# Edits at four block boundaries of a graph network with routed experts

## What is computed

```python
def _L1_gnn_ref(x, edge_index, edge_weight, W_conv, b_conv, W_lin, b_lin):
    n = x.shape[0]
    src, dst = (edge_index[0], edge_index[1])
    loop = jnp.arange(n, dtype=edge_index.dtype)
    src_f = jnp.concatenate([src, loop])
    dst_f = jnp.concatenate([dst, loop])
    w = jnp.concatenate([edge_weight, jnp.ones((n,), x.dtype)])   # the loops: an identity
    deg = jax.ops.segment_sum(w, dst_f, num_segments=n)
    dinv = jnp.where(deg > 0, jax.lax.rsqrt(deg), 0.0)
    norm = dinv[src_f] * w * dinv[dst_f]
    agg = jax.ops.segment_sum((x @ W_conv)[src_f] * norm[:, None], dst_f, num_segments=n) + b_conv
    return agg @ W_lin + b_lin
# L1_ffn: top-2 of 8 experts for each row; hidden 2048 with gelu; the two results mixed by gates
```

## Time and profile before

| what | us |
|---|---|
| median of three runs | 2176.21 (2175.12 to 2176.47) |
| the profiled execution | 2176.15 |
| its span | 2174.3 |
| PE busy | 1678.3 (77%) |
| DVE busy | 873.4 (40%) |
| POOL busy | 710.0 (33%) |
| ACT busy | 572.8 (26%) |
| seams between the blocks | 791.8, 1062.4, 1466.9 |

### The profile page before, as it was taken

The page is one execution under the profiler, slowest core; times in us unless marked ns, Lnnn a source line. Parts: engine busy times, 40 slices in busy tenths (PEclk is TensorE's granted clock), DMA queues, the critical chain, the costliest instruction groups (busy, mean ns, idle before and its releaser), DMA issues. The chain is left out here.

```text
span 2174.3 us, 25832 instructions
## 1 busy us (share of the span) xinstructions
PE 1678.3 (77%) x7876; PEld 1089.5 (50%) x7877; DVE 873.4 (40%) x2140; ACT 572.8 (26%) x1576; POOL 710.0 (33%) x803
## 2 busy tenths in 40 slices
PE   5111100269889978888898999979999999999998
PEld 4000000124335557777544444557777777777775
DVE  7101021124674579999897565660000000000002
ACT  0000001011112369999411111332212111222222
POOL 4777777700000039999730211012000000007004
PEclk8555555679999999999998999989999999999999
DMA  7000000000730030000204000447450440042003
GB/s 219 2 2 2 2 2 2 2 1 0 266 110 10 24 75 0 0 0 0 49 0 136 1 1 0 155 185 244 156 220 19 174 174 19 16 172 67 19 19 104
DMA packets 76132, 143.93 MB, mean 66 GB/s; under 512 B 21797, under 2 KB 23333, under 8 KB 71849
## 3 DMA queue, kind: packets, MB, share of 16 engines
q1 hardware_dynamic: 49415, 118.44, 15.6%
q0 software_dynamic: 18976, 10.95, 2.2%
q10 hardware_dynamic: 7682, 13.87, 1.9%
HBM read 107.61 MB, written 35.56 MB: 66 GB/s over the span
## 5 line engine op out<-in xcount | busy, mean ns | idle before, releaser
L2176 PEld LDWEIGHTS et_ps_h<-ex_turned,arena 128*128 128x128 f32 x3072 | 348.8, 193 | 17.1 <-issue 17.1
L2176 PE MATMUL et_ps_h<-ex_turned,arena 128*128 128x128 f32 x3072 | 349.1, 276 | 5.9 <-issue 5.9
L384 POOL DMA_INDIRECT sorted_edges<-fa_records,fa_edge_slot x313 | 309.6, 989 | 124.9 <-issue 101.6
L2186 PE MATMUL et_ps_y<-arena,et_hidden_t 128*128 x768 | 337.5, 592 | 0.0
L2086 DVE TENSOR_SCALAR ex_turned<-et_ps_t,ex_ln_g,ex_ln_b 128x128 f32<-128x128 f32 x96 | 32.8, 403 | 584.1 <-PE et_ps_t L2156 584.1
L1165 POOL TENSOR_SCALAR ad_row<-iota,ad_edges 128x128 fp32r<-128x128 f32 x360 | 235.6, 671 | 27.6 <-PE ad_ps L1235 23.8
L2186 PEld LDWEIGHTS et_ps_y<-arena,et_hidden_t 128*128 128x128 f32 x768 | 142.2, 190 | 160.7 <-issue 160.7
L517 PE MATMUL fa_banks<-arena 120*128 120x120 bf16 x216 | 33.4, 245 | 195.2 <-issue 195.2
L1214 ACT ACTIVATE ad_row_high<-ad_row,ad_edges 128x128 fp32r<-128x128 f32 x432 | 168.4, 390 | 8.1 <-POOL ad_row L1165 6.8
L1234 PE MATMUL ad_ps<-ad_to,ad_row_high 128*128 128x320 f32 x432 | 144.5, 345 | 32.2 <-ACT ad_row_low L1215 32.2
L2057 POOL DMA_INDIRECT xn_rows<-slot_out,from_slots x10 | 12.1, 1214 | 475.2 <-POOLq L2054 472.5
(11 more groups left out here) (421 smaller groups left out, 2245.0 us busy)
## 6 DMA issues: line engine op xcount, KB each, us to landing
arena<-L_ffn_W SPq DMA_DIRECT2D x16, 4096.0 KB, 13.5
slot_rows<-fa_zeros SPq DMA_DIRECT2D x1, 7424.0 KB, 26.3
slot_out<-fa_zeros SPq DMA_DIRECT2D x1, 7168.0 KB, 45.6
slot_out<-et_y ACTq DMA_DIRECT2D x24, 256.0 KB
et_rows_in<-slot_rows ACTq DMA_DIRECT2D x24, 256.0 KB, 2.7
sorted_edges<-fa_records,fa_edge_slot POOLq DMA_INDIRECT x313
arena<-x SPq DMA_DIRECT2D x1, 2240.0 KB
neighbour<-fa_Wv SPq DMA_DIRECT2D x10, 224.0 KB
```

The lines of the kernel that those rows point to most:

```text
L384: nc.gpsimd.indirect_dma_start(g.sorted_edges, bass.IndirectOffsetOnAxis(ap=self.edge_slot[0:rows, e:e + 1], axis=0), self.records[0:rows, ...
L2176: last = pe.matmul(ps_h[:, f % 2, i, :], x.weights[:, at:at + P], turned[:, k, :], start=(k == 0), stop=(k == KD - 1))
L2186: last = pe.matmul(ps_y[:], hidden_t[:, i, :], x.weights[:, bass.ds(buffer * (2 * HALF) + (HALF + i * D), D)], start=(i == 0), stop=(i == ...
```

## The change

- The first 24 chunks of the sorted edges are loaded by SP at the end of flow_attention, after its last stores, into a part of `arena` that is free then (`g.first_edges`); the load in the adjacency is gone, and `field` reads the new place for the first 8 groups. `first_loaded` now belongs to `g`.
- The ten identity adds stand behind the columns of group 1, ahead of the first sum, which waits for them (`chain`).
- ACT's part of the adjacency is written out for all 144 groups.
- `clear` sorts the numbers first.
- `buffer_of` is gone; PE computes `e % 2` in a register. The five semaphores that PE raised at its start are raised by SP.
- The output tiles' two DMAs are issued by two queues: of each tile, SP stores one part and ACT's queue the other, in alternation.

```diff
@@ Memory.clear
-        first = self.numbers[0]
-        for i, number in enumerate(self.numbers):
-            if i + 1 == len(self.numbers) or self.numbers[i + 1] != number + 1:
+        numbers = sorted(self.numbers)
+        first = numbers[0]
+        for i, number in enumerate(numbers):
+            if i + 1 == len(numbers) or numbers[i + 1] != number + 1:
                 self.nc.gpsimd.sem_clear(range(first, number + 1))
-                first = self.numbers[min(i + 1, len(self.numbers) - 1)]
+                first = numbers[min(i + 1, len(numbers) - 1)]
@@ flow_attention, SP
             sp.wait_ge(s["side_stored0"], 32 * T)
             sp.wait_ge(s["side_stored1"], 32 * T)
             sp.wait_ge(positions.s["zeroed"], 32)
+            sp.wait_ge(g.scattered, 16 * (FULL + 1))
+            sp.dma_start(g.first_edges[:], g.sorted_edges.rearrange("(p s) f -> p s f", p=P)[:, 0:FIRST * CHUNKS]
+                         ).then_inc(g.first_loaded, 16)
@@ adjacency
         def field(t, c, f):
             s = t * CHUNKS + c
+            if isinstance(t, int) and t < FIRST:
+                return g.first_edges[:, s, f:f + 1]
@@ adjacency, SP (POOL, DVE and ACT wait for g.first_loaded)
-            sp.dma_start(edges[:, 0:cut], sorted_edges[:, 0:cut]).then_inc(first_loaded, 16)
             sp.dma_start(edges[:, cut:], sorted_edges[:, cut:]).then_inc(loaded, 16)
@@ adjacency, DVE
+            def add_loops():
+                for b in range(T):
+                    own = weights[0:NT, b, b * NT:(b + 1) * NT]
+                    last = v.tensor_tensor(own, own, g.ident[0:NT, 0:NT], ALU.add)
+                last.then_inc(chain, 1)
 ...
                 last.then_inc(columns_made, 1)
+                if t == 1:
+                    add_loops()
 ...
+                if t == 0:
+                    dve.wait_ge(chain, 1)
                 dve.wait_ge(added, t + BUFS)
 ...
             dve.wait_ge(added, NG + BUFS)
-            for b in range(T):
-                own = weights[0:NT, b, b * NT:(b + 1) * NT]
-                last = v.tensor_tensor(own, own, g.ident[0:NT, 0:NT], ALU.add)
-            last.then_inc(chain, 1)
-            dve.wait_ge(chain, 1)
@@ adjacency, ACT
-            staggered(Steps(act, chain), 0, nothing, scale, nothing, NG, BUFS)
+            for t in range(NG):
+                scale(t, t % BUFS)
@@ nodes, DVE
-            c.link(v.tensor_scalar(x.buffer_of[:], x.expert_of[:], 1, None, ALU.bitwise_and))
@@ expert_tiles, SP
+            sp.sem_inc(s["rows_ready"], 1)
+            sp.sem_inc(s["hidden_ready"], 2)
+            sp.sem_inc(s["rows_turned"], 1)
+            sp.sem_inc(s["rows_loaded"], 16)
+            sp.sem_inc(s["tiles_done"], 1)
 ...
-            for t in range(0, T, 2):
+            for t in range(T):
+                cut = ROW_CUTS[t % 2]
                 sp.wait_ge(s["summed"], t + 1)
-                for cut in ROW_CUTS:
-                    sp.dma_start(A["out"][tile_rows(cut, t)], g.x[cut, t, :]).then_inc(s["out_stored"], 16)
+                sp.dma_start(A["out"][tile_rows(cut, t)], g.x[cut, t, :]).then_inc(s["out_stored"], 16)
@@ expert_tiles, ACT
-            for t in range(1, T, 2):
+            for t in range(T):
+                cut = ROW_CUTS[1 - t % 2]
                 act.wait_ge(s["summed"], t + 1)
-                for cut in ROW_CUTS:
-                    act.dma_start(A["out"][tile_rows(cut, t)], g.x[cut, t, :]).then_inc(s["out_stored"], 16)
+                act.dma_start(A["out"][tile_rows(cut, t)], g.x[cut, t, :]).then_inc(s["out_stored"], 16)
@@ expert_tiles, PE
-            pe.sem_inc(s["hidden_ready"], 2)
-            pe.sem_inc(s["tiles_done"], 1)
 ...
-            for n, amount in (("rows_loaded", 16), ("rows_turned", 1), ("rows_ready", 1)):
-                pe.sem_inc(s[n], amount)
             with used_tiles(pe) as t:
                 e = entry(pe, x.expert_of, t, EXPERTS - 1)
-                buffer = entry(pe, x.buffer_of, t, 1)
+                buffer = e % 2
```

More of the change, by code:

```diff
@@ L53 @@
 SLOTS_PER_P = NG * CHUNKS
+FIRST = 8
 ONE_HOT = T * BUCKET
@@ L541, in __init__ @@
         self.scattered, self.rows_scattered = m.sem("scattered"), m.sem("rows_scattered")
+        self.first_loaded, self.first_edges = m.sem("first_loaded"), None
         self.low_gathered, self.gathered = ([m.sem(f"{n}{t}") for t in range(T)] for n in ("low_gathered", "gathered"))
@@ L1117, in adjacency @@
     BUFS = 4
-    FIRST = 8
     with ExitStack() as stack:
@@ L1127, in adjacency @@
         weights = totals[:, 0]
-        first_loaded, loaded, columns_made, rows_made, scaled, used, added, chain, arrived = (m.sem(n) for n in (
-            "first_loaded", "loaded", "columns_made", "rows_made", "scaled", "used", "added", "chain", "arrived"))
+        loaded, columns_made, rows_made, scaled, used, added, chain, arrived = (m.sem(n) for n in (
+            "loaded", "columns_made", "rows_made", "scaled", "used", "added", "chain", "arrived"))
         block = stack.enter_context(nc.Block(no_gpsimd_drain=True))
@@ L1156, in _ @@
         def _(pool):
-            pool.wait_ge(first_loaded, 16)
+            pool.wait_ge(g.first_loaded, 16)
             def build_rows(t, u):
@@ L1173, in _ @@
             v = nc.vector
-            dve.wait_ge(first_loaded, 16)
+            dve.wait_ge(g.first_loaded, 16)
+            def add_loops():
[3 more added lines that the diff above has]
+                last.then_inc(chain, 1)
             def build_columns(t, u):
@@ L1197, in _ @@
             dve.wait_ge(added, NG + BUFS)
-            for b in range(T):
-                own = weights[0:NT, b, b * NT:(b + 1) * NT]
-                last = v.tensor_tensor(own, own, g.ident[0:NT, 0:NT], ALU.add)
-            last.then_inc(chain, 1)
-            dve.wait_ge(chain, 1)
         @block.scalar
         def _(act):
-            act.wait_ge(first_loaded, 16)
+            act.wait_ge(g.first_loaded, 16)
             def scale(t, u):
@@ L1257, in __init__ @@
         self.ln_g, self.ln_b = m.sb("ln_g", [P, KD]), m.sb("ln_b", [P, KD])
-        self.expert_of, self.buffer_of = m.sb("expert_of", [P, SLOT_TILES], I32), m.sb("buffer_of", [P, SLOT_TILES], I32)
+        self.expert_of = m.sb("expert_of", [P, SLOT_TILES], I32)
         self.loaded = {(u, part): m.sem(f"loaded{u}_{part}") for u in range(2) for part in ("up", "down")}
@@ L2212, in program @@
         g.x = rows
+        first_at = 2 * T * DST + T * D + D
+        g.first_edges = arena[:, first_at:first_at + FIRST * CHUNKS * 4].rearrange("p (s f) -> p s f", f=4)
         flow_attention(nc, A, g, arena)
```

## The result

| | us, median of 21 | lowest to highest |
|---|---|---|
| before | 2176.78 | 2170.66 to 2185.89 |
| changed | 2173.94 | 2167.46 to 2178.46 |

The ratio is 0.9975, with a 95% interval of 0.9966 to 0.9984: faster by 5.4 us, between 3.5 and 7.4. The two medians of the table alone would give 0.9987 and 2.8 us, the means 0.9977 and 4.9 us: executions lie so far apart that the figure depends on how they are averaged. On the 2176.21 from which the prediction started the ratio makes 2170.8, against 2169.3 forecast and a range of 2167.8 to 2172.9. The profiled execution of the changed kernel took 2169.2 with a span of 2167.4, as forecast (2169.27 and 2167.4).

What follows compares the result with a forecast made beforehand. DVE was taken to bound the adjacency and TensorE the expert tiles, so only seams and the end could gain: 1.25 + 2.1 + 0 + 1.92 + 1.41 + 0.2 = 6.88 us, giving 2169.3, range 2167.8 to 2172.9.

Steps and rivals of the forecast that it cites:

- Seam 1: Flow attention to adjacency: with the first edges loaded early, POOL starts 1.35 us sooner, less 0.1 for the adds: 1.25.
- The ten adds: Identity adds on DVE, moved ahead of the adjacency's first sum beside POOL's rows: 2.08 to 6.6 us, 3.3 taken.
- the middle value: Ten adds at two per POOL operation: 3.3 us, making the first sum 0.1 late.
- The low bound: Ten adds with no hindrance from POOL: 2.08 us, DVE ready 1.1 before the first sum falls due.
- the high value: Ten adds at one per POOL operation: 6.6 us, making the first sum 3.4 late.
- The first rival: One add per POOL operation at the adjacency's start: first sum 3.4 us late, whole time 2172.6; chance 22%.
- Seam 2: Adjacency to nodes: without the ten adds behind the last sum, the next block starts 2.1 us earlier.
- ACT written out: ACT's adjacency loop without loop registers: gains 0, since ACT has 0.09 us to spare per pair of groups.
- Seam 3: Nodes to experts: POOL's clears save 1.98 us, TensorE's start 1.45 plus a wait of 0.47; the smaller, 1.92.
- TensorE's part: Nodes to experts: semaphore raises moved to SP and a load replaced start TensorE's first tile 1.45 us earlier.
- The second rival: Nodes to experts: scatters held by DMA queues, not POOL's issue; that seam brings 0, whole time 2171.2; chance 9%.
- The end: End of the span: 24 clears become two for 1.41 us, the last tile's stores on two queues 0.2.

Runs made afterwards that it cites:

- e2: Changed kernel with the first edges' load back behind the barrier; first sum 8.35 us behind the barrier, last sum 267.50.
- e1: Changed kernel with the ten identity adds back behind the last sum; first sum 7.42 us behind the barrier, last sum to nodes' reduction 3.53 instead of 1.41.
- e7: Changed kernel with six more 128x320 additions on DVE behind the ten identity adds; first sum at 8.73 us instead of 7.29.
- e8: Changed kernel with DVE, not POOL, building one row of the first group; first sum at 6.60 us instead of 7.29, last sum 266.07 against 266.04.
- e9: Kernel before with only ACT's part of the adjacency written out; whole-time ratio 0.9997, first to last sum 258.55 us instead of 258.85.
- e3: Changed kernel with the clears unsorted again, TensorE's shorter start kept; first clear to turn of rows 31.19 us, 29.96 in the changed kernel.
- e4: Changed kernel with TensorE's start as before, sorted clears kept; first clear to turn of rows 30.98 us, 29.96 in the changed kernel.
- e5: Changed kernel with each tile's two output stores from one queue again; last sum to end 5.12 us, 4.65 in the changed kernel.

## Why the prediction was right

**Seam 1** (forecast 1.25, measured 1.02). What came out smaller is POOL's part: it started 0.69 behind the first clear and not 0.59, and its first three rows took 2.49 us in place of 2.27, the first alone 989 ns, where before none took over 871. The two together are 0.33 off 1.35; the adds, set at 0.1, cost nothing at the first sum, and 1.02 is left. e2 shows that the load was the cause of the old wait.

**The ten adds** (3.3 us by the middle value, measured 2.34). The low bound was nearer. In the 2.3 us of the adds, about three of them pass for each POOL operation, and POOL's take 708 to 773 ns. The rule on the shared port, from the Trainium skill's page "SBUF — State Buffer", section "Who interferes with whom", gave 6.6 and with it 2172.6. The page calls the shared ports an exclusive lock and says that a DVE instruction with two SBUF inputs contends with a GpSimd instruction that reads SBUF; that the later one is fully blocked stands there of DVE's 2-port modes. In this trace the rule held in the direction only: beside short POOL operations it is POOL that is slowed (597 to 710 and 974 ns), and DVE by 0.26 us in ten adds; no run here shows a DVE operation held for a whole row operation of POOL's. L1589, the row that gave the high value, has a POOL operation of some 3 us against it. The first rival is refuted by e1 and by DVE's 1.37 us of wait. The statement behind it, that a late first sum is not given back, holds for e7 by the end of the block; but the like does not hold for an early one (e8).

**Seam 2** (2.1, measured 2.12, and 2.12 again in e1): right in mechanism and size.

**ACT written out** (0, measured 0.3 in e9): ACT was not the bound, yet the pair of groups became 0.002 shorter, 72 times. That makes 0.14, and the rest is of no certain origin. My argument excluded a gain because DVE was busy all the time. Busy is not the same as working at its own speed: one and the same column operation takes DVE between 366 and 493 ns in this block. That a change in when ACT comes round shifts this pace, through TensorE and POOL, is argued, not shown.

**Seam 3** (1.92, measured 1.58; on the faster chips 1.15 to 1.97, against e9). Right that each saving alone is worth little, and that both together make the wait of 0.47 go (e3, e4), though e9 shows the same place with a wait of 0.02 only, so that the 0.47 was in part that execution's. The price of TensorE's part was right, 1.42 for 1.45, POOL's too large: from first clear to first scatter it was 3.33 and is 1.49, 1.84 instead of 1.98, since one clear of 29 numbers takes 197 ns where one of a single number took 44; the other long one was there before, with 243 ns. The term that was missed is the clock: the first group ran at 1.2 GHz for a microsecond more and took 0.48 us longer. The second rival, rows held by the DMA queues, would have kept the landing of the second tile's rows at its old place, 31.01 to 31.49 behind the first clear with unsorted clears (before, e3, e9). With sorted clears it came at 28.54 to 30.01 in eight executions. The means, 31.2 and 29.3, differ by 1.9, about POOL's whole 1.84: the rival is refuted, and the queues leave a scatter of some tenths up to 1.5 us.

**The end** (1.61; 2.23 in the pair of profiles, about 1.8 over the executions). Clears 1.30 for 1.41, as one clear of 23 numbers takes 154 ns where one of a single number took 38; the split 0.5 for 0.2.

**Whole**: 6.88 forecast, 6.94 in the pair of profiles, 5.4 (3.5 to 7.4) over the runs of one chip and 5.7 over those of another. Taking the stretches as the runs leave them, 1.1 to the last sum, then 2.1, 1.6 and 1.8, one gets 6.6, inside both intervals (the second is 3.3 to 8.1) and in the upper part of both. The mechanism was right at every seam; that the whole came out within 0.1 in the pair of profiles is owed to terms that cancelled.

## What to carry to other kernels

Work that must run once can be put into a wait that exists anyway, but look how long the wait is and what runs beside it: here 2.3 us of adds vanished in a wait of 2.8, and 2.8 us more, put where 1.4 of waiting was left, made the first sum 1.4 late. Where two engines lead to the same place behind a barrier, shorten both or neither: alone the edits were worth 0.56 and 0.35 us at most, and about nothing against e9, together 1.2 to 2.0. And where executions differ by more than the effect, cut the trace into stretches between events and compare those; the second seam's 2.12 us was the same to 0.01 in every kernel, while whole times of one kernel spread over 10 us.

## What the runs showed of the hardware that I had not expected

**The same kernel took 2176 and 2181 us where the result and e5 to e8 were measured, and 1833 and 1832 on the two chips of the other experiments.** Nearly all of it is ahead of the first seam: the first clear comes at 792 in the one case, at 448 to 451 in the other. In a window of 50 us inside the scatter of the edges (busy us and count: PE, PEld, DVE, ACT, POOL; granted clock), the kernel before as profiled for the prediction, and e1:

```profile
100.00:150.00 50.00, 5.25 (x18) 1.86 (x18) 0.42 (x3) 0.00 (x0) 38.11 (x40) 0.50 0.03 2
```

```profile
100.00:150.00 50.00, 50.00 (x129) 22.59 (x128) 20.82 (x32) 8.61 (x14) 38.12 (x40) 1.00 0.03 2
```

POOL does the same, 38.1 us in 40 instructions. TensorE in the slower case issues one product every 2.8 us, without a wait that the trace can name (changed kernel):

```profile
102.10 0.26 PE L519 MATMUL fa_banks<-arena 120*128 120x120 bf16 x1 [2.54 <-issue]
104.90 0.26 PE L519 MATMUL fa_banks<-arena 120*128 120x120 bf16 x1 [2.54 <-issue]
```

In e1 TensorE has long been through these and is in the attention's products at full clock. Why its instructions come so slowly in the other case is not settled. The stretch also carries a good part of the scatter between executions: there the first clear came between 788.6 (e7) and 797.6 (e5), on the faster chips within 2.2 us of one another. What lies there, 340 us, is fifty times what this change was about.

**An engine's operation beside another's is not slowed evenly.** Beside six DVE additions of 320 columns with two SBUF operands POOL's row operation went from 597 to 974 ns, and DVE took 0.46 us from one to the next. Beside POOL operations of 3 us, in the nodes, it was one of DVE's that took 3155 ns for 752.

**A clear of many semaphores costs more than one of a few, and far less than as many clears of one.** With the sizes that follow from the kernel's semaphore numbers, one clear took 38 to 44 ns for a single number, 68 for 8, 86 for 9, 154 for 23, 197 for 29, 242 for 40 and 480 for 81. From one single clear to the next it is 0.065 to 0.071 us. So two of them replace thirty for 1.84 us less.
